# Relative values of a vision transformer: four head pairs per matmul, four queries in the column groups, and identity matmuls that restore the order

## The reference

```python
rv2 = rel_v[idx]                                   # idx[q, k] = clip(k - q, -68, 68) + 68
attn = softmax((attn1 + attn2) / sqrt(c))
w1 = jnp.einsum('bhqk,bhkd->bhqd', attn, rv)
w2 = jnp.einsum('bhqk,qkd->bhqd', attn, rv2)       # one 65 x 16 matrix for each query position q
out = (w1 + w2).transpose(0, 2, 1, 3).reshape(b, t, c)
```

## Time and profile before

| | us |
|---|---|
| median of 3 runs (lowest, highest) | 252.2 (252.07, 254.18) |
| span of the profiled execution, first to last instruction | 249.9 |
| median less that span: what lies around it | 2.3 |
| PE, DVE, ACT, POOL busy | 230.9, 191.3, 164.2, 62.8 |
| start of the first `relative` | 115.54 |
| start of `up(0, 0)` and of `up(0, 1)` | 135.28 and 139.16 |
| end of the routing scores | 149.28 |

### The profile page before, as it was taken

How to read it: one execution, slowest core, us unless ns; L and a number is a source line. 1 busy time by engine, 2 the same in 40 slices (tenths; PEclk the granted TensorE clock), 3 DMA queues, 4 the chain that set the end, 5 groups by cost and what they waited for, 6 DMA issues and landing times.

```text
span 249.9 us, 6298 instructions
## 1 busy us (share of the span) xinstructions
PE 230.9 (92%) x2316; PEld 194.7 (78%) x2316; DVE 191.3 (77%) x481; ACT 164.2 (66%) x509; POOL 62.8 (25%) x94
## 2 busy tenths in 40 slices
PE   1999999999998889989989999999899999999993
PEld 1945665899776766658778899889799999999972
DVE  1576789865668899998186738678999989989991
ACT  2461469752199899993026987422799888898870
POOL 8814132096005465469112400000000000000000
PEclk9999999999999999999999999999999999999999
DMA  6980000000003326064000000069888510001011
GB/s 147 335 217 3 1 0 1 3 3 0 3 0 81 91 65 108 4 212 129 3 7 3 0 3 0 8 103 131 151 211 260 173 37 10 22 4 32 0 42 34
DMA packets 15625, 16.46 MB, mean 66 GB/s; under 512 B 1747, under 2 KB 14367, under 8 KB 15468
## 3 DMA queue, kind: packets, MB, share of 16 engines
q1 hardware_dynamic: 14424, 15.59, 26.0%
q0 software_dynamic: 544, 0.35, 0.6%
q10 hardware_dynamic: 628, 0.14, 0.3%
HBM read 13.91 MB, written 2.16 MB: 64 GB/s over the span
## 4 chain that ended last, share of the span: by engine, by line
PE 54%; DVE 13%; issue 11%; POOL 11%; DMA 4%; ACT 3%; SPq 2%; DVEq 0%; POOLq 0%
PE banks L1328 49%; POOL region_e L471 5%; DMA region_d<-in_L_tok_W_sw 4%; DVE KT L1286 2%; POOL w_lo L526 2%; DVE top L1028 1%; DVE stb L992 1%; POOL region_d L478 1%; PE banks L1531 1%; POOL rstd L413 1%; PE banks L1672 1%; DVE stb L911 1%; ACT region_d L701 1%; DVE y_lo L1269 1%; DVE stats L890 1%
## 5 line engine op out<-in xcount | busy, mean ns | idle before, releaser
L760 ACT ACTIVATE w_sb<-banks,vecs 128x416 f32<-128x416 f32 x60 | 36.4, 608 | 11.2 <-PE banks L1328 8.9
L677 ACT ACTIVATE region_e<-banks,ntop 128x64 f32<-128x64 f32 x128 | 38.3, 346 | 5.0 <-DVE ntop L1035 4.8
L768 ACT ACTIVATE y_hi<-w_sb 128x416 fp32r<-128x416 f32 x60 | 32.7, 548 | 8.1 <-DVE w_sb L1260 8.1
L1269 DVE TENSOR_TENSOR y_lo<-w_sb,y_hi 128x416 fp32r<-128x416 f32 x60 | 34.9, 585 | 1.0 <-ACT y_hi L768 1.0
L677 ACT ACTIVATION_READ_ACCUMULATOR region_e<-banks,ntop 128x1 f32 x128 | 29.8, 238 | 0.0
L1328 PE MATMUL banks<-x_hi,w_hi 128*128 128x416 f32 x80 | 29.3, 366 | 0.0
L1328 PE MATMUL banks<-x_lo,w_hi 128*128 128x416 f32 x80 | 28.1, 352 | 0.0
L1328 PE MATMUL banks<-x_hi,w_lo 128*128 128x416 f32 x80 | 28.0, 350 | 0.0
L1260 DVE TENSOR_TENSOR w_sb<-w_sb,region_c 128x416 f32<-128x416 f32 x40 | 23.4, 586 | 2.5 <-ACT w_sb L760 1.0
L1328 PE MATMUL banks<-y_hi,w_hi 128*128 128x416 f32 x60 | 22.3, 371 | 1.5 <-DVE KT L1286 1.0
L1328 PE MATMUL banks<-y_hi,w_lo 128*128 128x416 f32 x60 | 21.1, 351 | 0.0
(11 more groups left out here) (238 smaller groups left out, 502.1 us busy)
## 6 DMA issues: line engine op xcount, KB each, us to landing
region_c<-out SPq DMA_DIRECT2D x4, 832.0 KB, 14.3
xnT<-out SPq DMA_DIRECT2D x5, 208.0 KB, 13.7
QT<-out SPq DMA_DIRECT2D x5, 208.0 KB, 14.1
region_a<-in_x SPq DMA_DIRECT2D x2, 512.0 KB, 5.3
region_a<-in_x SPq DMA_DIRECT2D x1, 1024.0 KB, 9.5
out<-h SPq DMA_DIRECT2D x2, 512.0 KB, 5.8
h<-out SPq DMA_DIRECT2D x4, 256.0 KB, 5.0
w_sb<-in_L_ffn_W SPq DMA_DIRECT2D x1, 1024.0 KB, 5.6
```

Source lines behind the costliest of these rows:

```text
L677: last = a.activation(dst[:, h // 2, h % 2], src[:, h // 2, h % 2], ACT.Exp, scale=SCALE, bias=ntop[:, o + h:o + h + 1], accum_out=esum[:, ...
L760: a.activation(lifted(u), bank[h_bank(i)][:, 0:FB], ACT.Gelu, bias=vecs[:, b:b + 1])\
L768: a.activation(h_hi(u), lifted(u), ACT.Copy).then_inc(S["hi_ok"], 1)
L1269: v.tensor_tensor(h_lo(u), lifted(u), h_hi(u).bitcast(F32), ALU.subtract).then_inc(S["lo_ok"], 1)
```

## The change

`relative(n)` now takes, for each query, all four head pairs at once as 128 moving columns (`PT[:, :, :, q]`, all 260 bytes apart), and puts four neighbouring queries into the four column groups. Its result has the query where the head pair should be. ACT copies it to `region_d` (`evac_rel`), and `regroup(n)` moves it by 16 matmuls whose weights are 32 columns of the identity, into the bank that DVE adds from. With that go new PSUM banks, a new order of PE and DVE, two evacuations of probabilities moved from DVE to ACT, the rounding of the expert matrices cut in two parts on ACT and POOL, and some semaphores made into one.

```diff
-OP_BANKS = (1, 2, 3, 5)
-REL_BANKS = (4, 5, 6, 0)
+OP_BANKS = (0, 1, 4, 5)
+REL_BANKS = (2, 3, 2, 3)
...
+        RVq = region_d[:, 0:TOK].rearrange("p (t j b) -> p t j b", t=PAIRS, j=PJ)
...
-            sp_.wait_ge(S["d_out"], 16 * 18)
+            sp_.wait_ge(S["d_out"], 16 * 21)
...
-            pool.wait_ge(S["w1hi_ok"], 1)
-            g.tensor_tensor(w1_lo[:, :], w1_sb[:, :], w1_hi[:, :].bitcast(F32), ALU.subtract).then_inc(S["w1_split"], 1)
+            def split_up(part, cols):
+
+                pool.wait_ge(S["w1hi_ok"], part + 1)
+                g.tensor_tensor(w1_lo[:, cols], w1_sb[:, cols], w1_hi[:, cols].bitcast(F32), ALU.subtract)\
+                    .then_inc(S["w1_split"], 1)
+
+            split_up(0, slice(0, DIRECT * FH))
...
             deviation2(4)
+            split_up(1, slice(DIRECT * FH, E * FH))
...
+            for p in range(PAIRS - 2, PAIRS):
+                act.wait_ge(S["pt_ps"], p + 1)
+                a.activation(PT[:, :, 2 * p:2 * p + 2, 0:NPATCH],
+                             bank[prob_bank(p)][:, :].rearrange("p (j b q) -> p j b q", j=PJ, b=2), ACT.Copy)\
+                    .then_inc(S["ptA_ok"], 1)
             act.wait_ge(S["d_fw1"], 16)
-            a.activation(w1_hi[:, :], w1_sb[:, :], ACT.Copy).then_inc(S["w1hi_ok"], 1)
+            a.activation(w1_hi[:, 0:DIRECT * FH], w1_sb[:, 0:DIRECT * FH], ACT.Copy).then_inc(S["w1hi_ok"], 1)
+
+            def evac_rel(n):
+
+                act.wait_ge(S["rv_ps"], n + 1)
+                a.activation(RVq[:, 4 * n:4 * n + 4].rearrange("p t j b -> p (t j b)"), bank[4 + n % 2], ACT.Copy)\
+                    .then_inc(S["rv_ok"], 1)
+
+            for n in range(NBLK):
+                evac_rel(n)
+            a.activation(w1_hi[:, DIRECT * FH:], w1_sb[:, DIRECT * FH:], ACT.Copy).then_inc(S["w1hi_ok"], 1)
...
-            act.wait_ge(S["d_out2"], 48)
...
             probs(PAIRS - 3)
-            probs(PAIRS - 2)
-            probs(PAIRS - 1)
...
             attended(0)
+            residual(0)
             attended(1)
-            residual(0)
             attended(2)
             residual(1)
             attended(3)
+            attended_class()
             low(0)
-            attended_class()
             residual(2)
+            residual(3)
             low(1)
-            residual(3)
...
-                    for j in range(PJ):
-                        last = mm(bank[REL_BANKS[n]][32 * j:32 * j + 32, i * IMG:(i + 1) * IMG],
-                                  RVBD[:, 32 * (63 - q):32 * (63 - q) + 32], PT[:, j, :, q])
+            def relative(n):
+
+                if n == 0:
+                    pe.wait_ge(S["pt_ok"], PAIRS - 2)
+                    pe.wait_ge(S["ptA_ok"], 2)
+                if n >= 2:
+                    pe.wait_ge(S["rv_ok"], n - 1)
+                for t in range(TPB):
+                    for f in range(4):
+                        q = 16 * n + 4 * t + f
+                        last = mm(bank[4 + n % 2][32 * f:32 * f + 32, t * P:(t + 1) * P],
+                                  RVBD[:, 32 * (63 - q):32 * (63 - q) + 32], PT[:, :, :, q])
+                last.then_inc(S["rv_ps"], 1)
+
+            def regroup(n):
+
+                pe.wait_ge(S["rv_ok"], n + 1)
+                if n >= 2:
+                    pe.wait_ge(S["o_ok"], n - 1)
+                o = bank[REL_BANKS[n]][:, :].rearrange("p (t f b) -> p t f b", t=TPB, f=4)
+                for f in range(4):
+                    for d in range(4):
+                        last = mm(o[32 * d:32 * d + 32, :, f, :], ident[:, 32 * f:32 * f + 32],
+                                  RVq[:, 4 * n:4 * n + 4, d, :])
+                last.then_inc(S["w2_ps"], 1)
...
-            relative(0, range(0, 4))
+            turn_pc(7)
             for p in range(PAIRS - 4, PAIRS - 2):
                 values(p)
-            relative(0, range(4, 8))
-            turn_pc(7)
+            keep_warm(1, spare=2)
+            relative(0)
             for p in range(PAIRS - 2, PAIRS):
                 values(p)
-            filled(0, late)
-            filled(1, early)
+            relative(1)
+            regroup(0)
+            relative(2)
             project(0)
-            relative(1, late)
-            relative(2, early)
+            regroup(1)
+            relative(3)
             project(1)
-            relative(2, late)
-            relative(3, early)
+            regroup(2)
+            regroup(3)
+            relative_class()
+            turn2(0)
             project(2)
-            turn2(0)
-            relative(3, late)
-            relative_class()
-            pe.wait_ge(S["h1_ok"], 1)
-            keep_warm(2, spare=1)
             project(3)
             pe.wait_ge(S["oc_ok"], 1)
-            mm(bank[6][0:IMG, 0:C], OTc, wo).then_inc(S["opc_ps"], 1)
+            mm(bank[6][0:IMG, C:2 * C], OTc, wo).then_inc(S["opc_ps"], 1)
             pe.wait_ge(S["w1_split"], 1)
-            pe.wait_ge(S["o_ok"], 4)
+            pe.wait_ge(S["h1_ok"], 2)
             pe.wait_ge(S["xlo_ok"], 1)
             up(0, 0)
             turn2(1)
+            pe.wait_ge(S["o_ok"], 4)
+            up(1, 0)
+            pe.wait_ge(S["h1_ok"], 3)
             router(0)
-            pe.wait_ge(S["h1_ok"], 3)
-            up(1, 0)
+            keep_warm(2, spare=4)
             pe.wait_ge(S["xlo_ok"], 2)
             up(0, 1)
             turn2(2)
...
             down(0, 3)
+            pe.wait_ge(S["w1_split"], 2)
             up(DIRECT, 0)
```

## The result

| | us |
|---|---|
| before: median of 20 runs (lowest, highest) | 251.85 (250.76, 254.26) |
| after: median of 20 runs (lowest, highest) | 253.69 (252.61, 257.61) |
| ratio, 95% interval | 1.0074 [1.0047, 1.0102] |
| span of the profiled execution, before and after | 249.9, 250.5 |

The change makes the kernel 0.7% slower, some 1.9 us, where the prediction had 0.1 us faster. The median lies 0.4 us above the upper end of the range.

The account below looks back on a forecast made before the run. PE sets the pace up to `up(0, 1)`, DVE once PE gets shorter; following the new order put `up(0, 1)` at 139.05 against 139.16. Span 249.9 - 0.1 + 2.3 = 252.1 us, range 249.1 to 253.3.

Parts of the forecast that it names:

- POOL's second piece of `w1_lo`: POOL after deviation2(4): 3.4 us, about 141 to 145, costed at 0, bounds -0.1 and +0.1 us.
- handover or wait that this schedule misses: Anywhere in the followed schedule: a missed handover or wait, by more than the other cases; chance 0.04.
- One for one after `up(0, 1)`: From up(0, 1), 139.16 before, to the end: everything moves with its start by the same amount.
- The scattered round: In relative: four matmul rows of 128 scattered columns take 218 ns, bounds 178 to 245, weighing 24 times; chance 0.58.
- `relative(0)`: On PE after turn_pc(7), values of two pairs and a filler: starts at 116.6.
- `regroup`: On PE after relative: 0.87 us each, 32 rounds at 109 ns in all, output runs of 32 at the adjacent price.
- PE idle before `project(1)`: PE waits there for attended(1), which DVE does behind residual(0) and ends at 127.5.
- DVE without a gap: DVE from attended(2) at 129.6 to the end of low(1) at 139.0: 9.4 us without a wait.
- `up(0, 1)` released by `x_lo`: PE's up(0, 1) starts near 139.1, released by x_lo, with PE itself ready at about 138.5.
- The first (scattered columns cost nothing): In relative: scattered columns cost the adjacent 109 ns a round, 2.6 us less than before, 249.6 us; chance 0.25.
- The second (the clock falls in the stretch of `relative`): PE's clock falls in the stretch of relative, making the kernel slower; chance 0.08.
- The third (`low(0)` late behind ACT): DVE's low(0) waits for ACT when 0.4 us of cover goes; a whole 1.49 us would give 253.2; chance 0.05.

Follow-up runs that it names:

- runs 5: Kernel with the change and w1's roundings in one piece, relative reading 128 adjacent columns (wrong choice of probabilities): 249.61 us, ratio 0.9864.
- run 7: Kernel with the change and w1's roundings in one piece, each relative block with another column spacing (three leave out the right probabilities): 251.74 us, one execution.
- run 4: Kernel with the change, POOL's second piece of w1's rest made in six instructions of 256 columns at the same place: 259.05 us, ratio 1.0214.
- run 1: Kernel with the change, w1's roundings in one piece again: 252.86 us; repeated side by side, unaltered with two pieces 253.81 us, one piece 252.48 us.
- run 3: Kernel before, only w1_lo made by POOL in two pieces, the second behind the deviation of block 2: 260.19 us, ratio 1.0323.
- run 8: Kernel with the change, probabilities of a pair's two images side by side: one piece 248.73 us, ratio 0.9898; last, two pieces 251.31 us, ratio 0.9968.

## Why the prediction was wrong

**The step that failed** is the one that costed POOL's second piece of `w1_lo` at 0 with bounds of 0.1 us: "runs after `deviation2(4)`, about 141 to 145, and `up(DIRECT, 0)`, which waits for it, stands behind the routing in PE's queue". Time and place were right (139.99 to 143.44, with 1.01 added 141.0 to 144.5), and so was the wait: `up(DIRECT, 0)` didn't wait for it. What was missing is the question whom the instruction itself keeps from SBUF while it runs. It cost 1.69 us on DVE (2.38 less 0.69). None of the rivals named it; it falls under the "handover or wait that this schedule misses". The opening's sentence that queues are held back only by semaphores is wrong at the same point: `low(2)` stands as running from 141.62 and was held all the same. Without the piece the kernel takes 252.86 and 252.48 us, inside the range; so the rest of the sum held nearly as it was.

The timeline of the kernel before showed the mechanism already, in the probabilities, some 33 us ahead of `low(2)`:

```profile
109.14 1.04 POOL L471 TENSOR_TENSOR region_e<-region_e,rsum 128x512 f32<-128x512 f32 x1 [1.19 <-DVE rsum L1009]
...
109.29 1.44 DVE L1016 TENSOR_TENSOR region_e<-region_e,rsum 128x512 f32<-128x512 f32 x1
```

POOL's multiplication ends at 110.18 and DVE's at 110.73, 0.55 us later, as in every 128x512 case above. A 128x512 operation on DVE that takes twice its usual time beside a POOL row is what to look for.

**One for one after `up(0, 1)`** therefore failed as well, between `up(0, 1)` (+0.41) and `up(0, 2)` (+2.09). Behind that place it held up to the routing scores (+2.09).

**The scattered round** was right as a mechanism and a little small: 218 ns in the sum, 228 measured, inside 178 to 245. Twenty-four times 10 ns are 0.24 us of the 0.52 by which `up(0, 1)` came later than forecast (139.57 against 139.05). Of the rest, some 0.3, about 0.16 have come by `project(0)`, which starts at 123.70 where the sum gives 123.3, of which the rounds explain 0.24; another 0.14 come between `project(1)` and `attended(2)` (126.89 to 129.13, 2.24 us, where the sum has 2.1). What makes them isn't shown.

**Right by the rows of after:** `relative(0)` at 116.59 (forecast 116.6); `regroup` 0.89 (0.87), so output runs of 32 columns cost nothing extra; PE idle before `project(1)`, released by `attended(1)`, though only 0.17; DVE without a gap, 9.37 us from `attended(2)` to the end of `low(1)` (9.4); `up(0, 1)` released by `x_lo`.

**The rivals.** The first (scattered columns cost nothing) is refuted by blocks of 1.85 us and by the runs 5 and 7. Its price was well worked out all the same: 2.6 us on the path, and with adjacent columns and the piece out of the way 2.86 come off it; the ratio is 0.9864 [0.9785, 0.9943], where the rival's 249.6 is 0.990 of 252.2. The second (the clock falls in the stretch of `relative`) didn't happen there; PE's clock is at its upper level in every slice up to the last. The third (`low(0)` late behind ACT) didn't happen: `low(0)` starts with no idle time before it.

## What to carry to other kernels

A POOL operation whose result nobody waits for is not free: look at what DVE does while it runs, and if that has both operands in SBUF, count the rest of POOL's row as its delay. For moving columns of a matmul, count the 16-byte lines that they touch as well as the columns: two float32 to a line cost little more than four (114 to 126 ns a round against 109), one to a line twice as much, and a layout that puts two neighbours side by side can serve a reader along either axis.

## What the runs showed of the hardware

- The hold between POOL and DVE is exact, and the profile shows it as busy time of the one that is held, not as a wait: DVE's 128x512 operation ends 0.55 to 0.56 us after POOL's (143.44 and 144.00, 141.67 and 142.22, 110.18 and 110.73), however long it has waited. It goes the other way too: POOL's small product at 133.18 in after takes 0.47 us instead of 0.20 while `low(0)` runs.
- POOL operations that follow each other without a wait hold DVE to the end of the last (run 4, one profile).
- A line of 16 bytes costs the moving side of a round of four column groups 1.8 ns (run 7, one execution; 231 ns for 128 lines in after too).
- PE's clock can fall after an idle time of 1.64 us (3.5 us at 1.2 GHz in run 1, and likewise in the last profile of run 8) and need not (the profile of after); after 3.04 us it fell for nine (run 3). So a wait of PE of this size has a price that differs from execution to execution, and a longer one can cost more than twice its own length.
